# Image and text tokens through attention and experts on one NeuronCore: products over 192 inputs as 64-row pairs

## The reference, cut to what matters

```python
h = tokens_of_images(x)                    # 8 images, 64 tokens each, D = 192
h = concat([h, text_embedding(...)], 1)    # + 128 text tokens: 8 sequences of L = 192
# block 1, 12 heads of 16
xn = ln(ln(h))
qkv = xn @ attn_qkv_w + b;   qkv2 = xn @ ssm_qkv_w + b2
ao = softmax(q k' / 4, window of 64) v  @ attn_proj_w
so = linear_attention(elu(q2) + 1.0001, elu(k2) + 1.0001, v2) @ ssm_out_w
x2 = x + (ao + ln(so)) @ out_w
h = h + x2 + gelu(ln(x2) @ mlp_w1) @ mlp_w2          # 192 -> 768 -> 192
# block 2, on x3 = ln(h): 1536 tokens
shared = mean over 2 experts of (silu(x3 @ wg) * (x3 @ wu)) @ wd       # 192 -> 768 -> 192
routed = top 2 of 16 experts of the same form, weighted
out = h + shared + routed
```

## Time and profile before

| | |
|---|---|
| runs (3) | median 761.47 us, 760.28 to 761.68 us |
| profiled execution | 762.45 us, of it 760.8 us span |
| TensorE busy (PE) | 734.8 us, 97% of the span |
| weight loads (PEld) | 523.3 us, 69% |
| VectorE (DVE), ScalarE (ACT), GpSimd (POOL) | 301.0, 237.6, 213.5 us |
| stages: before the loop, loop, tail, routed, end | 113.7, 238.3, 141.0, 215.0, 52.8 us |
| TensorE busy in each stage | 107.8, 228.3, 139.4, 214.0, 45.3 us |

### The profile page before, as it was taken

One profiled execution on the slowest core, in us unless ns is written; L12 is line 12 of the kernel. 1 busy time (PEld: TensorE's weight loads), 2 busy tenths in 40 slices (PEclk: granted clock), 3 DMA queues, 4 the chain that ended last, 5 costly groups with the idle time before them and its releaser, 6 DMA issues.

```text
span 760.8 us, 17118 instructions
## 1 busy us (share of the span) xinstructions
PE 734.8 (97%) x6954; PEld 523.3 (69%) x6954; DVE 301.0 (40%) x804; ACT 237.6 (31%) x515; POOL 213.5 (28%) x284
## 2 busy tenths in 40 slices
PE   8999899999999999999999999999999999999996
PEld 7447665666676766657545763688889889788544
DVE  1345576656546727535322752212112211121233
ACT  0202442555546455462332201112212222122110
POOL 5536114663232321310010046111111111111263
PEclk9999999999999999999999999999999999999999
DMA  8600000900000000000000026199999999994132
GB/s 315 256 0 2 3 0 1 341 15 2 2 2 2 2 2 2 3 2 2 1 0 1 1 87 260 42 380 379 354 366 346 361 342 372 338 361 183 30 87 83
DMA packets 33485, 101.38 MB, mean 133 GB/s; under 512 B 4873, under 2 KB 19726, under 8 KB 28048
## 3 DMA queue, kind: packets, MB, share of 16 engines
q1 hardware_dynamic: 23472, 68.92, 24.9%
q0 software_dynamic: 9952, 31.60, 11.1%
HBM read 90.66 MB, written 9.83 MB: 132 GB/s over the span
## 4 chain that ended last, share of the span: by engine, by line
PE 90%; DVE 5%; issue 2%; ACT 1%; DMA 1%; SPq 0%; DVEq 0%; ACTq 0%
PE PS L1586 14%; PE PS L2382 9%; PE PS L2247 8%; PE PS L2261 6%; PE PS L2386 5%; PE PS L2249 4%; PE PS L2398 3%; PE PS L2350 2%; PE PS L1592 2%; PE PS L1598 2%; PE PS L2403 2%; PE PS L1668 1%; PE PS L2020 1%; PE PS L2026 1%; PE PS L1884 1%
## 5 line engine op out<-in xcount | busy, mean ns | idle before, releaser
L1544 DVE TENSOR_TENSOR rh<-rsg,PS 128x768 f32<-128x768 f32 x32 | 30.5, 954 | 158.4 <-ACT rsg L996 158.4
L2382 PE MATMUL PS<-xt,w_rgu 128*128 128x128 f32 x576 | 70.1, 276 | 1.0 <-ACT rsg L996 1.0
L2382 PEld LDWEIGHTS PS<-xt,w_rgu 128*128 128x128 f32 x576 | 67.5, 192 | 3.1 <-issue 3.1
L996 ACT ACTIVATE rsg<-PS 128x768 f32<-128x768 f32 x32 | 25.9, 810 | 132.5 <-PE PS L2386 101.8
L2247 PE MATMUL PS<-X,w_sgu 128*128 128x512 f32 x132 | 64.3, 609 | 0.1
L661 POOL DMA_DIRECT2D y_slots<-ys x32 | 17.6, 549 | 156.3 <-ACT ys L988 156.3
L1586 PE MATMUL PS<-w_rdn,rh 128*128 128x192 f32 x288 | 50.9, 327 | 0.0
L1586 PEld LDWEIGHTS PS<-w_rdn,rh 128*128 128x128 f32 x288 | 46.2, 190 | 0.4 <-issue 0.4
L816 ACT ACTIVATE pb<-sm,nm 128x128 f32<-128x128 f32 x144 | 42.1, 372 | 12.6 <-DVE nm L1334 12.5
L2247 PEld LDWEIGHTS PS<-X,w_sgu 128*128 128x128 f32 x132 | 22.8, 190 | 30.9 <-issue 28.4
L563 POOL TENSOR_TENSOR rs<-ve,minus_half 128x3 f32<-128x3 f32 x12 | 10.4, 870 | 118.8 <-DVE ve L1257 118.8
(11 more groups left out here) (394 smaller groups left out, 1464.9 us busy)
## 6 DMA issues: line engine op xcount, KB each, us to landing
w_rgu<-in_wgu SPq DMA_DIRECT2D x24, 1152.0 KB, 8.0
w_pgu<-in_wgu SPq DMA_DIRECT2D x16, 1152.0 KB, 7.4
w_rdn<-in_wd POOLq DMA_DIRECT2D x22, 576.0 KB, 6.7
w_pdn<-in_wd POOLq DMA_DIRECT2D x16, 576.0 KB, 6.3
x_slots<-zeros SPq DMA_DIRECT2D x1, 3072.0 KB, 19.3
xs<-x_slots SPq DMA_DIRECT2D x32, 96.0 KB, 4.6
y_slots<-ys POOLq DMA_DIRECT2D x32, 96.0 KB, 5.8
w_sgu<-in_shared_gu SPq DMA_DIRECT2D x2, 1152.0 KB
```

The costliest lines, as they stand in the source:

```text
L996: act.activation(rsg[:, j, :], PS[:, 0:2, :].rearrange("p a b -> p (a b)")[:, 0:FF], ACT.Silu).then_inc(S["r_sg"], 1)
L1544: dve.tensor_tensor(rh[:, j, :], rsg[:, j, :], PS[:, 2:4, :].rearrange("p a b -> p (a b)")[:, 0:FF], ALU.mult).then_inc(S["r_h"], 1)
L2382: pe.matmul(dst(y, m), w[:, y, 128 * m:128 * m + 128], xt[:, j, y, :], start=(m % 4 == 0), stop=False, skip_group_check=True)
```

## The change

Every product over 192 inputs of the pair loop and of the shared units takes one form: six 64-row matmuls, the two sides a and b beside each other on the two row halves and in two banks, three after one another (c = 0, 1, 2). The weights are laid out for this on the host. For it X gets a third plane, with plane 1's upper 64 rows in its lower half and plane 0's lower 64 rows in its upper half. GpSimd copies it for the first pair (two copies ahead of the power for the third pair), SyncE by DMA for the other three, ahead of the shared weights' loads, and again for each pair when its new inputs for the shared units are there. For `widen` VectorE copies the third plane into mix (`residual_rest`), at the end of step j = 3 and in the tail between gate-times-up of units 8 and 9. New waits on x_rest stand on TensorE, GpSimd and SyncE. In the first group of step j = 0, `turn_heads` and VectorE's `heads_out` come after the product, no longer inside it. The routed experts are as before.

```diff
+SIDES = (slice(0, DR), slice(DR, DM))
...
-        X = sb("X", [128, 2, NTOK])
+        X = sb("X", [128, 3, NTOK])
...
 (SyncE's program)
-            sp.wait_ge(S["p_zT"], 4)
+            def move_rest(at):
+                sp.dma_start(X[0:DR, 2, at], X[DR:128, 1, at]).then_inc(S["x_rest"], 16)
+                sp.dma_start(X[DR:128, 2, at], X[0:DR, 0, at]).then_inc(S["x_rest"], 16)
+            sp.wait_ge(S["x_rest"], 2)
+            sp.wait_ge(S["p_xn"], 4)
+            move_rest(slice(PT, NTOK))
             for e in range(E_S):
                 sp.dma_start(w_sgu[:, e, :, :], a["shared_gu"][e]).then_inc(ld_moe, 16)
...
+            for p in range(PAIRS):
+                sp.wait_ge(S["c_x3s"], p + 1)
+                sp.wait_ge(S["x_rest"], 32 * p + 34)
+                move_rest(slice(PT * p, PT * p + PT))
...
 (GpSimd's program)
                 image_power(i, 2)
+            pool.wait_ge(S["p_rs2"], 4)
+            pool.wait_ge(S["p_xn"], 3)
+            pool.tensor_copy(X[0:DR, 2, 0:PT], X[DR:128, 1, 0:PT]).then_inc(S["x_rest"], 1)
+            pool.wait_ge(S["x_rest"], 1)
+            pool.tensor_copy(X[DR:128, 2, 0:PT], X[0:DR, 0, 0:PT]).then_inc(S["x_rest"], 1)
+            pool.wait_ge(S["x_rest"], 2)
             image_power(2, 1)
...
 (ScalarE, residual_turned)
-                for c in range(2):
+                for c in (1, 0):
...
 (VectorE)
+            def residual_rest(p):
+                dve.wait_ge(S["z2_out"], 3 * p + 2)
+                dve.tensor_copy(mix[0:DR, :], zX[DR:128, 1, :])
+                dve.tensor_copy(mix[DR:128, :], zX[0:DR, 0, :]).then_inc(S["z2_out"], 1)
...
+                elif j == 3 and q >= 1:
+                    residual_rest(p)
...
-            gate_times_up(7, 9)
+            gate_times_up(7, 8)
+            residual_rest(p)
+            gate_times_up(9, 9)
...
 (TensorE, project; project_values alike)
-                pe.matmul(PS[:, a, 0:PT], w_qk[:, k, 0, :], X[:, 0, at], start=True, stop=False, skip_group_check=True)
...
-                pe.matmul(PS[:, b, 0:PT], w_qk[:, k, 1, :], X[:, 1, at], start=True, stop=False, skip_group_check=True)
...
-                pe.matmul(PS[:, a, 0:PT], w_qk[DR:128, k, 2, :], X[DR:128, 1, at], start=False, stop=True, skip_group_check=True
...
-                pe.matmul(PS[:, b, 0:PT], w_qk[0:DR, k, 2, :], X[0:DR, 0, at], start=False, stop=True, skip_group_check=True
...
+                for c in range(3):
+                    if p == 0 and c == 2:
+                        pe.wait_ge(S["x_rest"], 2)
+                    for bank, rows in zip(banks, SIDES):
+                        if c == 0 and bank == banks[1] and second is not None:
+                            second()
+                        mm = pe.matmul(PS[:, bank, 0:PT], w_qk[rows, k, c, :], X[rows, c, at], start=(c == 0), stop=(c == 2),
...
 (TensorE, shared units)
+            def unit(banks, e, m, tokens):
+                for c in range(3):
+                    for bank, rows in zip(banks, SIDES):
+                        mm = pe.matmul(PS[:, bank, :], w_sgu[rows, e, c, 128 * m:128 * m + 128], X[rows, c, tokens],
+                                       start=(c == 0), stop=(c == 2))
+                mm.then_inc(S["e_up"], 1)
...
 (TensorE, widen)
+                planes = (zX[:, 0, :], zX[:, 1, :], mix[:, :])
                 for k in range(3):
...
+                    for n, c in enumerate((1, 0, 2)):
+                        if k == 0:
+                            pe.wait_ge(S["z2_out"], 3 * p + n + 1)
+                        for side, rows in enumerate(SIDES):
+                            if k >= 1 and n == 0 and side == 1:
+                                pe.wait_ge(S["up_out"], p * FM + 2 * k - 1)
+                            mm = pe.matmul(PS[:, UP_BANKS[2 * k + side], 0:PT], w_m1[rows, k, c, :], planes[c][rows, :], start=(n == 0),
...
 (TensorE, the step)
-                    project(q, 2, (5, 6), sums_read, (lambda: turn_heads(3 * q - 1)) if q >= 1 else None)
+                    project(q, 2, (5, 6), sums_read)
+                    if q >= 1:
+                        turn_heads(3 * q - 1)
...
+                        pe.wait_ge(S["x_rest"], 34 + 32 * 2)
                         last_unit(0)
...
+                    if e == 0 and m == 0 and s >= 1:
+                        pe.wait_ge(S["x_rest"], 34 + 32 * (s + 2))
+                    unit((n % 2, 2 + n % 2), e, m, slice(512 * s, 512 * s + 512))
...
 (host)
+    def sides(low, high):
+        low, high = (w.reshape((3, DR) + w.shape[1:]).swapaxes(0, 1) for w in (low, high))
+        return np.ascontiguousarray(np.concatenate([low, high[:, [1, 2, 0]]], 0))
```

More of the change, by code:

```diff
@@ L101, in build @@
         ident = sb("ident", [128, 128])
-        ones = sb("ones", [1, 512])
+        ones = sb("ones", [1, 128])
         cols = sb("cols", [128, NCOL])
@@ L187, in build @@
             up_mm up_out dn_mm c_hx h2_read c_ve3 c_rs3 c_x3 c_x3T c_x3s c_go c_lg c_ls c_ex
[L188 removed]
+            d_m d_cnt d_slot x_rest scattered
             e_up e_sg e_gu e_dn e_acc o_done
@@ L313, in build @@
         yg = (h_sb, tb3("yg", [128, NT, D]))
+        chosen = tb3("chosen", [128, TOPK, NT, E_R])
+        weight = tb3("weight", [128, TOPK, NT])
         scr3.close()
@@ L1234, in project_out @@
                     odd_queries(2, a, slice(0, DR))
+                    between()
                     phi_linear(p, 2, a, slice(DR, 128))
@@ L1830, in project_values @@
             def project_values(p, s, banks, second=None):
-                a, b = banks
                 first = PT * p + L * s
-                head, tail = slice(first, first + 128), slice(first + CH, first + L)
-                pe.matmul(PS[:, a, 0:2 * D], X[:, 0, head], w_v[:, 0, :], start=True, stop=False, skip_group_check=True)
-                if second is not None:
-                    second()
-                pe.matmul(PS[:, b, 0:2 * D], X[:, 1, tail], w_v[:, 1, :], start=True, stop=False, skip_group_check=True)
@@ L1839, in project_values @@
-                pe.matmul(PS[:, a, 0:2 * D], X[DR:128, 1, head], w_v[DR:128, 2, :], start=False, stop=True, skip_group_check=True
-                          ).then_inc(S["v_mm"], 1)
-                pe.matmul(PS[:, b, 0:2 * D], X[0:DR, 0, tail], w_v[0:DR, 2, :], start=False, stop=True, skip_group_check=True
-                          ).then_inc(S["v_mm"], 1)
+                for c in range(3):
+                    if p == 1 and s == 0 and c == 2:
+                        pe.wait_ge(S["x_rest"], 34)
+                    for bank, rows, at in zip(banks, SIDES, (slice(first, first + 128), slice(first + CH, first + L))):
+                        if c == 0 and bank == banks[1] and second is not None:
+                            second()
+                        mm = pe.matmul(PS[:, bank, 0:2 * D], X[rows, c, at], w_v[rows, c, :], start=(c == 0), stop=(c == 2),
+                                       skip_group_check=True)
+                        if c == 2:
+                            mm.then_inc(S["v_mm"], 1)
@@ L1946, in linear_values @@
                 mm.then_inc(S["lo_mm"], 1)
[L1948 to L1953 removed]
+            def unit(banks, e, m, tokens):
+                for c in range(3):
+                    for bank, rows in zip(banks, SIDES):
+                        mm = pe.matmul(PS[:, bank, :], w_sgu[rows, e, c, 128 * m:128 * m + 128], X[rows, c, tokens],
+                                       start=(c == 0), stop=(c == 2))
+                mm.then_inc(S["e_up"], 1)
+            def last_unit(n):
+                unit((5, 6), 0, n, slice(0, 512))
             def turn_heads(G):
@@ L2462, in pairs, with side_pairs @@
                                               for k in range(w.shape[1] // 2)], 1))
+    def sides(low, high):
+        low, high = (w.reshape((3, DR) + w.shape[1:]).swapaxes(0, 1) for w in (low, high))
+        return np.ascontiguousarray(np.concatenate([low, high[:, [1, 2, 0]]], 0))
+    def side_pairs(w):
+        return np.ascontiguousarray(np.stack([sides(w[:, 2 * k], w[:, 2 * k + 1]) for k in range(w.shape[1] // 2)], 1))
     def shared_rows(v):
```

73 lines of the change are left out of this document (22 added, 51 removed).

## The result

The changed kernel takes 757.0 us in the median of five runs (756.63 to 757.88) against 760.54 us of the kernel before, measured beside it (five runs, 760.28 to 761.68): a ratio of 0.995 (of the mean times, here and below), interval 0.9937 to 0.9963, 3.5 us. Forecast were 7.6. The time lies in the range given (747.5 to 758.8) and the sign was right, but the size was less than half.

A forecast was written before the change was run, and what follows sets the result against it. TensorE was taken to bound the kernel (90% of the chain). Gains of 1.0 + 0.4 + 0 + 4.95 + 1.35 = 7.7 us off the profiled 762.45 gave 754.75, as a median 753.9; range 747.5 to 758.8.

The forecast's parts named there:

- rival C: Gains less: `widen` loses 0.8 us in each of four pairs, the start gains 0.3; 757.8 us, chance 0.16.
- Price of a change of form: Each TensorE change between 128-row and 64-row passes costs 0.20 us; 77 fewer give 15.4 if nothing else ends last.
- Rival E: Slower: weights for the same row half are not loaded while that half computes; 14 us more, 776 us, chance 0.07.
- Start: Up to and with the first pair's products: 8 changes, 1.6 us, less one wait of some 0.55; gain 1.0.
- Loop: Pair loop outside `widen`, 1 + 6 changes: 0.2 us at q=0, 0.2 at q=3, together 0.4.
- `widen`: Loop's three `widen`, 15 changes, 3.0 us on paper: gelu ends last, so gain 0.
- Tail: Shared units and products beside them after the loop, 34 changes, 6.8 us on paper: gain 4.95, bounds 3.6 and 6.8.
- Where only TensorE's list decides, I count 0.2 each: Tail units 10 to 11, 13 to 14, 18 to 23, 24 to 26: 0.2 us a change, together 3.6.
- End: End of the kernel, 13 changes, 2.6 us on paper: capped by the gathers at 1.39, less a hop, gain 1.35.
- The gathers cap it: At the end, the last gather lands at 752.57, so only 1.39 us can be gained unless the gathers move.
- Rival D: No measurable change: routed stage runs by weight loads, TensorE waits; only the end's 1.35 us left, 760.1, chance 0.08.
- Rival B: Whole gain: gelu and the gathers are no bound; 15 us less 2 for waits, 748 us, chance 0.11.

The follow-up runs named there:

- the early copies: Changed kernel with GpSimd's two copies of the first pair's third plane ahead of the second power of the image statistics: 760.49 us, ratio 0.9996.
- the run with the old form: Changed kernel with `widen` alone back in its old form, without VectorE's copies into mix: 757.22 us, ratio 0.9955.
- units old: Changed kernel with the shared units alone back in the form of 128-row and 64-row products: 759.57 us, ratio 0.9998.
- old with the halves swapped: Changed kernel with shared units in their old form, their two 64-row products in the other order, rows 64 to 127 last: 759.47 us, ratio 0.9983.
- mixed version: Changed kernel with shared expert 1's units in the old form, expert 0's in the new one, and GpSimd's copies early: 757.25 us, ratio 0.9957.

## Why the prediction was right or wrong

*The range.* That the time lies in the range is owed to the range's reach up to rival C: the forecast's own range ended at 756.5, and the median is 757.0. Of the 7.7 added up, the profiled execution lacks 3.1, by three terms: 1.7 for the clock, 1.35 in the tail and 0.5 at the end, less 0.4 that start and loop gave beyond their sizes.

*Price of a change of form: right.* Six units in 15.65 without a disturbance are 2.58 each, 0.40 under the earlier trace rows.

*Rival E: fell.* The run of units 18 to 23 without the scatter has 36 slots on the same two halves in 15.65 us, 0.43 each: the loads are hidden. The Trainium skill ("TensorE: Matmul & The Clock Gate", Part 3: Packing small matmuls) says that a weight load overlaps only matmuls of another row group; the trace disagrees.

*Start, forecast 1.0: 1.1.* The third plane was waited for once: the loads stood for 0.74, and the early copies gave TensorE 0.4 back, round the 0.55 worked out. The sum had no term for the clock, and one stretch at the lower level more than in the kernel before cost the profiled execution 1.7, the largest single miss.

*Planes of the other pairs, forecast 0: 0.* No product of pair 1 waits for its plane in the profile.

*Loop, forecast 0.4: 0.65*, of it 0.3 up to the end of the first `widen`.

*`widen`, forecast 0: 0.* From 204.21 to 211.42 it takes 7.21, against 7.15, and the run with the old form agrees. The rows below, of all engines, answer to the earlier trace rows:

```profile
204.66 0.36 DVE L1335 COPY mix<-zX 64x384 f32<-64x384 f32 x1 [0.28 <-ACT zX L859]
205.03 0.35 DVE L1336 COPY mix<-zX 64x384 f32<-64x384 f32 x1
205.44 0.36 PEld L2052 LDWEIGHTS PS<-mix,w_m 64*128 64x128 f32 x4 [0.28 <-DVE mix L1336]
...
206.42 1.05 ACT L867 ACTIVATE hT<-PS,cols 128x384 f32<-128x384 f32 x2 [0.28 <-PE PS L2052]
207.05 0.62 PEld L2052 LDWEIGHTS PS<-zX,w_m 64*128 64x128 f32 x5 [0.64 <-ACT hT L867]
```

Gelu starts 2.21 after `widen`'s first product, 2.41 before, and releases the next group's load 0.63 later, as before. The round as a whole is not shorter, so what the five changes of form a pair would have saved was waited for.

*Tail, forecast 4.95: 3.6.* This is the step that failed: "Where only TensorE's list decides, I count 0.2 each", with 10 changes, 2.0, for units 18 to 23. They gave 0.95 up to the products down behind them. TensorE's timeline of the kernel before there:

```profile
458.25 1.88 PE L2247 MATMUL PS<-X,w_sgu 128*128 128x512 f32 x4
...
475.98 4.17 PE L2261 MATMUL PS<-w_sdn,gu 128*128 128x192 f32 x24
```

These 17.73 us became 16.78 in the change, and 15.65 without the scatter, 2.08 less: there the list did decide, as forecast. Beside the scatter a unit also waits for the late signal of the one but one before, and the 1.1 that unit 23 stood are missing from the 2.0. The whole tail, from the loop's last scores to xs, takes 139.76 before, 136.16 in the change and 134.96 without the scatter, 4.8 less; TensorE's timeline of that run:

```profile
349.14 0.67 PE L1882 MATMUL PS<-km,qm 32*64 32x128 f32 x16
...
484.10 0.33 PE L1610 MATMUL PS<-ident,xs 128*128 128x128 f32 x1
```

So the term that was left out is the signal's delay, put at nothing without a reason. The other pieces came within 0.2 of their sizes: 0.9 at units 24 to 26, 0.4 each at 10 to 11, at 13 to 14 and at w_so with units 4 and 5, 0.5 at 15 to 17, 0.2 at 7 to 8, 0.1 at unit 9 with `widen`.

*End, forecast 1.35: 0.83, and by another cause.* "The gathers cap it" failed, and was misread already in the kernel before: VectorE's last sums stood there behind a sum that waited for TensorE's products down:

```profile
753.30 0.62 DVE L1430 SCALAR_TENSOR_TENSOR acc<-PS,acc 128x192 f32<-128x192 f32 x2 [3.21 <-PE PS L2261]
```

TensorE's and GpSimd's timelines of the changed kernel:

```profile
729.43 8.00 PE L1975 MATMUL PS<-X,w_sgu 64*128 64x512 f32 x36 [0.83 <-issue]
737.86 2.85 PE L1975 MATMUL PS<-X,w_sgu 64*128 64x512 f32 x12 [0.44 <-DVE gu L1443]
```

```profile
745.50 0.94 POOL L688 DMA_INDIRECT yg<-y_slots,slot  x1 [0.30 <-issue]
```

The last gather was issued 4.47 earlier than in the earlier trace rows, as it follows the routed stage, and landed at 748.1; the last sums, at 749.40, waited for the products down again. Units 30 to 35 took 17.45 (before 17.74), where the six without a disturbance took 15.65. What took the gain is the wait at 729.43, for a gate-times-up that stands behind the first gathers' sums on VectorE, and the wait at 737.86 behind the late signal of unit 33.

*Rival D: fell*: xs is used 3.73 earlier and the end comes 4.56 earlier, so the routed stage gave nothing back. *Rival B fell*: `widen` and the late signals ended last beside TensorE's list. *Rival C* named nearly the time measured (757.8), but by `widen` and the start, and neither lost anything. The sum over the profiled executions: 1.1 at the start, 0.65 in the loop, 3.6 in the tail, 0.8 at the end, less 1.7 for the clock: 4.5 of 4.57.

## What to carry to other kernels

Making neighbouring products one form is worth its 0.20 us a change where TensorE's list alone sets the pace; where another engine's answer to the product but one before is needed, price the round trip with its signal beside the list: in units 18 to 23 a signal 1.94 late cost 1.1, so only some 0.8 of delay was to spare. A fill or a tile that shrinks moves what starts behind it: look at the first microseconds of a diff too. Measure on a second chip before a gain of half a per cent is believed.

## What was not expected of the hardware

A product's completion can reach the other engines long after the product: in the six-pair form the signal came 1.9 us late in the profile of the change while a batch of scatters drained, and 6.5 us late on another chip, until the last gather had landed, and 6.4 on a further one in the run without the scatter; in the form with 128-row passes no unit was late beside the same transfers (four kernels: before, units old, old with the halves swapped, and expert 1 of the mixed version). TensorE went on with its next passes meanwhile, so the delay is in the signal. Why the form matters is open, and so is why some executions show so much more of it: the changed kernel's own runs on the second chip go from 756.82 to 763.35 us.

One kernel's executions differ in TensorE's clock: with 13 spare products one took 754.88 us at a mean clock of 0.997, with no low clock but at the end, and another 758.02 us at 0.995. The profile of the change has two stretches at 1.2 GHz before its end, that of the kernel before one. Neither more spare products nor a later start did away with them. What TensorE did before does not tell the executions apart: ahead of the stretch at 68.4 us in the kernel before it had been busy 3.40 of 3.40 us (65.0 to 68.4), and the profile with the scatter's waits moved has the same 3.40 there and a clock of 1.00 behind it.
